# Causal attention in a fused two-layer block: the later keys masked on TensorE, the second half of the queries first, its rough maxima one group ahead

## The chip, the core and the metric

The kernel is one program on one core of one Trainium2 chip. The engines named below are PE (TensorE, matrix products into PSUM), DVE (VectorE), ACT (ScalarE), POOL (GpSimd) and SP (SyncE, which here issues DMAs). The metric is the device time of one execution in microseconds; shorter is better. "Before" is the kernel without the change.

## What is computed

The program runs a mixture of experts, attention, a mixture of experts, a low-rank layer, a second attention of another kind, and a low-rank layer, each added to the running rows `x`. The change touches the first attention alone. Its input is 2 sequences of 1024 tokens with 256 features, 16 heads of 16 features:

```python
q = (x @ Wq).reshape(B, T, H, Dh)            # B, T, H, Dh = 2, 1024, 16, 16
k = (x @ Wk).reshape(B, T, H, Dh)
v = (x @ Wv).reshape(B, T, H, Dh)
scores = jnp.einsum('bthd,bshd->bhts', q, k)
scores = scores * mask                       # mask = tril of ones
attn = jax.nn.softmax(scores / T ** 0.5, axis=-1)
out = jnp.einsum('bhts,bshd->bthd', attn, v).reshape(B, T, H * Dh)
return out @ Wo
```

The mask multiplies. A later key has the score 0, not minus infinity, and so still has a weight in the softmax.

## The kernel before

`attention_stage` works in 8 groups `G` (`NG`): 4 heads (`HG`) of one sequence. Queries are taken in two halves `q` of 512 (`HB`), keys in 8 tiles `j` of 128 (`P`, `TB`). A group is a hand-written loop of 24 slots `s` (`NSL`). Slot `s` handles key tile `s // 2` in the order of `key_of` for one pair of heads: `scores_of` (L984) makes the scores with keys on the partitions, ACT takes the exponential (`exp_of`, L1149) into `PT`, POOL zeroes the part above the diagonal (`cut_later_keys`, L861), and at every odd slot `values_of` (L1002) adds the key tile's values into PSUM bank 6. The first query half has 4 key tiles (slots 0 to 7), the second 8 (slots 8 to 23). Each key tile of a half that crosses the diagonal uses fewer of the 512 queries (512, 384, 256, 128).

The exponential needs the maximum of each query over its keys. It comes from a rough pass over the same products with the queries on the partitions: `rough_scores` (L963) makes a piece of up to 512 columns in bank 0 or 1 in turn, and `maxima` on DVE (L1258, L1260) reduces it; PE may be two pieces ahead. A piece that ends on the diagonal is multiplied by a mask row `SEEN` while it is reduced, one head at a time (L1258); a piece wholly below the diagonal is a plain `tensor_reduce` (L1260). A group has 40 pieces, 12 for its first half and 28 for its second. `per_slot` says how many stand in a slot: slots 8 to 23 of group G make the first half of group G+1 and 16 pieces of its second half, slots 0 to 5 of group G+1 the 12 that are left. Then for each half: `block_max` on DVE (L1270 to L1273), four transposes on PE (`max_rows`, L972) into bank 7 (`MISC`), and copies of four rows into `QT` (`max_copies`, L1132 on ACT, L1280 on DVE), which let `scores_of` subtract the maximum inside the product. For the first half this stands in slots 16 and 17 of the group before; for the second half in slot 6 of its own group, and slot 8 is the first that needs it.

`MISC` is also used by projections (L946), by filler work in the slots of `FILL` (transposes and values of the second sequence, the output projection of the first) and by `out_transposes` (L1010). Each user waits until the reader of the last one is done (`misc`).

The queries and keys of a group are projected two groups ahead, split into a high and a low part (`high`, `low`), and SP places the 16 rows of each head into `QT` and `KT` with DMAs (L835). Group 0 has 24 DMAs of 512 tokens, every later group 12 of 1024 tokens, from the end of the group two before. DVE clears the maximum rows of `QT` for the next group in slots 7 and 14 (`clear_max_rows`, L1286), four `memset`s a group. Ahead of group 0, in the prologue, the first 28 pieces of group 0 run alone; after group 7 the output rows of the second sequence are projected.

Each engine runs its instructions in the order in which they are written; semaphores are the only link between engines.

## Time and profile before

| what | us |
|---|---|
| median of 3 runs | 2196.66 |
| lowest and highest of the 3 | 2193.28, 2201.62 |
| the profiled execution | 2202.58 |
| its span, first to last instruction | 2200.8 |
| groups 0 to 7 of the attention, 339.25 to 712 of the span | 372.8 |

The rows further down come from the profiled execution. A time in a row is counted from the start of the span; `<-` in square brackets names what ended the idle time before an instruction, `x4` how many like it follow each other. A matmul's time in a row includes the time until its end is visible, so matmuls that follow each other overlap: the distance of two starts is what one costs. PEclk is the granted share of TensorE's full clock; the records hold two levels of it, 1.2 and 2.4 GHz.

### The profile page before, as it was taken

To read this page: it belongs to the slowest core of one execution; us is meant where nothing else is said; L and a number is where in the kernel's file an instruction comes from. 1 tells how busy PE (TensorE), PEld (TensorE's weight loads), DVE (VectorE), ACT (ScalarE), POOL (GpSimd) and SP (SyncE) were. 2 spreads that over 40 slices of the span, in tenths; PEclk is the share of its full clock that TensorE was granted. 3 is DMA by queue.
4 is the path that set the end of the run, shared out by engine and by line. 5 is a ranking of instruction groups with operands and counts; after the bars stand their busy time and mean duration, and the time that the engine had idled before them with its cause. 6 is when DMAs were issued, how large, how long until landed. Compare 5 with 4: busy or idle time off the path is not lost. (4 is left out here: it accounts for less than half of the span.)

```text
span 2200.8 us, 29601 instructions
## 1 busy us (share of the span) xinstructions
PE 1992.3 (91%) x8700; PEld 1251.4 (57%) x8700; DVE 1277.8 (58%) x3064; ACT 817.6 (37%) x1549; POOL 866.3 (39%) x684
## 2 busy tenths in 40 slices
PE   5899869898888789977689999999999999999987
PEld 5676635554554766656545555555565555555556
DVE  6322275777775822227556666666656666667526
ACT  2122244555555212223224444444514444444423
POOL 0344301231212044432025555665425555565632
PEclk9999968999899689998669999999999999999999
DMA  9111232232220811224232212222122222211101
GB/s 389 48 63 63 56 124 29 30 48 39 29 30 1 339 62 60 67 72 155 47 72 58 54 42 51 57 57 57 23 64 58 53 58 57 55 44 47 31 1 51
DMA packets 60587, 150.91 MB, mean 69 GB/s; under 512 B 12976, under 2 KB 18304, under 8 KB 58176
## 3 DMA queue, kind: packets, MB, share of 16 engines
q1 hardware_dynamic: 50208, 120.43, 20.9%
q0 software_dynamic: 9120, 24.92, 3.6%
q10 hardware_dynamic: 1152, 4.19, 0.5%
q8 instruction: 60, 0.98, 0.2%
q14 instruction: 47, 0.39, 0.1%
HBM read 68.95 MB, written 18.61 MB: 40 GB/s over the span
## 5 line engine op out<-in xcount | busy, mean ns | idle before, releaser
L1843 POOL TENSOR_TENSOR mla_PS<-mla_PS,mla_PT 128x1024 f32<-128x1024 f32 x192 | 458.1, 2386 | 199.5 <-ACT mla_PT L2129 198.1
L2272 DVE TENSOR_REDUCE mla_MXP<-PS 128x1 f32<-128x512 f32 x512 | 334.6, 687 | 200.5 <-PE PS L1924 198.3
L2129 ACT ACTIVATE mla_PT<-PS 128x512 f32<-128x512 f32 x512 | 293.5, 599 | 420.6 <-PE PS L1944 372.5
L1953 PE MATMUL PS<-mla_PT,mla_CN 128*64 128x512 f32 x1024 | 274.2, 614 | 0.0
L522 DVE COPY moe_HT<-PS 128x256 f32<-128x256 f32 x188 | 70.7, 418 | 301.5 <-PE PS L648 301.5
L1924 PE MATMUL PS<-mla_KH,mla_QH 113*128 113x512 f32 x512 | 199.4, 456 | 18.1 <-DMA mla_KL<-mla_SL 17.9
L1944 PE MATMUL PS<-mla_QH,mla_KH 113*128 113x512 f32 x512 | 210.2, 411 | 1.7 <-ACT mla_QH L2113 1.5
L1944 PE MATMUL PS<-mla_QH,mla_KL 113*128 113x512 f32 x512 | 201.8, 394 | 0.0
L1944 PE MATMUL PS<-mla_QL,mla_KH 113*128 113x512 f32 x512 | 201.7, 394 | 0.0
L684 POOL DMA_INDIRECT moe_XS<-rows_in,moe_GI x96 | 93.5, 974 | 268.3 <-PE PS L634 132.0
L1149 ACT ACTIVATE att_PT<-PS 128x1024 f32<-128x1024 f32 (+1 forms) x192 | 152.1, 812 | 94.3 <-PE PS L984 92.7
L1924 PEld LDWEIGHTS PS<-mla_KH,mla_QH 113*128 113x128 f32 x512 | 91.3, 194 | 168.2 <-DVE mla_MXP L2272 89.7
L641 PE MATMUL PS<-W,moe_ST 128*128 x376 | 174.9, 608 | 1.9 <-DVE moe_ST L516 1.9
L656 PE MATMUL PS<-W,moe_HT 128*128 x752 | 173.7, 384 | 1.4 <-DVE moe_HT L522 1.4
L1843 POOL TENSOR_TENSOR mla_PS<-mla_PT 128x1024 f32<-128x1024 f32 x32 | 76.3, 2384 | 249.1 <-ACT mla_PT L2129 249.1
L963 PE MATMUL PS<-att_KT,att_QT 128*128 128x512 f32 (+3 forms) x384 | 145.6, 423 | 22.6 <-DVE att_MX L1260 10.1
L656 PEld LDWEIGHTS PS<-W,moe_HT 128*128 128x128 f32 x752 | 138.9, 190 | 22.8 <-issue 1.8
L1258 DVE CUSTOM_DVE_ANT_0 PS<-PS,att_SEEN 128x128 f32<-128x128 f32 (+3 forms) x256 | 122.8, 508 | 46.9 <-PE PS L963 44.3
L861 POOL TENSOR_SCALAR_AFFINE_SELECT att_PT<-att_PT 128x256 f32<-128x256 f32 x128 | 51.9, 406 | 244.6 <-ACT att_PT L1149 244.6
L2284 DVE RECIPROCAL PS<-PS 128x128 f32<-128x128 f32 x128 | 108.7, 918 | 52.3 <-PE PS L1960 52.3
L1944 PEld LDWEIGHTS PS<-mla_QH,mla_KH 113*128 113x128 f32 x512 | 96.4, 188 | 68.3 <-issue 22.0
L963 PEld LDWEIGHTS PS<-att_KT,att_QT 128*128 128x128 f32 x384 | 74.7, 210 | 100.5 <-DVE att_MX L1260 38.5
(295 smaller groups left out, 3188.8 us busy)
## 6 DMA issues: line engine op xcount, KB each, us to landing
W<-in_W_dram SPq DMA_DIRECT2D x16, 2048.0 KB, 27.9
mla_QH<-mla_SH SPq DMA_DIRECT2D x64, 128.0 KB, 2.4
mla_KH<-mla_SH SPq DMA_DIRECT2D x64, 128.0 KB, 2.4
mla_QL<-mla_SL SPq DMA_DIRECT2D x64, 128.0 KB, 2.5
mla_KL<-mla_SL SPq DMA_DIRECT2D x64, 128.0 KB, 2.4
mla_KH<-mla_SH SPq DMA_DIRECT2D x64, 96.0 KB, 2.3
mla_KL<-mla_SL SPq DMA_DIRECT2D x64, 96.0 KB, 2.4
sums_Y<-rows_out SPq DMA_DIRECT2D x9, 512.0 KB, 6.2
```

The source lines that it names most:

```text
L641: ins = pe.matmul(bank(2 + u)[:, :], ST[:, u, k, :], g.W1[:, expert, k, :], start=(k == 0), stop=(k == KD - 1))
L656: ins = pe.matmul(bank(6 + u)[:, 0:D], HT[:, u, k, :], W2[:, expert, k, :], start=(k == 0), stop=(k == KF - 1))
L963: ins = pe.matmul(out[:, m, :], QT[:, H % 2, h, i * P:(i + 1) * P], KT[:, H % 2, h // 2, k0:k0 + w], start=(m == 0), stop=(m == len(hs) - 1))
L1149: act.activation(PT[:, kk % 2, 2 * pair:2 * pair + 2, c0:HB], st_banks(s)[:, :, c0:HB], ACT.Exp, scale=SEQ ** -0.5).then_inc(s_p.handle, 1)
L1258: ins = dve.tensor_tensor_reduce(part, part, seen, 1.0, LEAST, ALU.mult, ALU.max, MX[:, q, c, h, t:t + 1])
L1843: pool.tensor_tensor(PS[:, :], PT[:, slot(0), :] if k == 1 else PS[:, :], PT[:, slot(k), :], ALU.add).then_inc(s_ps.handle, 1)
L1924: pe.matmul(bank(piece_bank(n))[:, :], QH[USED, buf, h, tile * P:(tile + 1) * P], KH[USED, buf, h, c * HB:(c + 1) * HB], start=True, stop= ...
L1944: ins = pe.matmul(bank(st_bank(s, h))[:, :], kk[USED, buf, h, ks], qq[USED, buf, h, qs], start=(n == 0), stop=(n == 2))
L1953: ins = pe.matmul(bank(6)[h * DKVL:(h + 1) * DKVL, :], CN[:, b, k, 0:DKVL], PT[:, slot(k), h * HB:(h + 1) * HB], start=(k == 0), stop=(k = ...
L2129: act.activation(PT[:, slot(k), h * HB:(h + 1) * HB], bank(st_bank(s, h))[:, :], ACT.Exp, scale=MLA_SCALE).then_inc(s_p.handle, 1)
L2272: dve.tensor_reduce(MXP[:, n // NPC, c, h, t:t + 1], bank(piece_bank(n))[:, :], AX_X, ALU.max).then_inc(s_mx.handle, 1)
L2284: dve.reciprocal(bank(A)[:, cols], bank(A)[:, cols]).then_inc(s_rc.handle, 1)
```

## The change

- Masking. `SEEN` goes. PE adds to each diagonal piece a product of an identity (`IDR`) with a matrix `LATER` that is 0 or -1e30, over the last 128 columns of each head, into the same bank. DVE reduces every piece with one plain `tensor_reduce`, over 4 heads (128 columns each), 2 heads (256) or 1 head at once. A group has 38 pieces, 11 and 27.
- Order. Slots 0 to 15 take the second query half (all 8 key tiles), slots 16 to 23 the first half. The pieces of the second half of group G+1 stand in slots 6 to 20 of group G, those of its first half in slots 21 to 23 and in its own slots 0 to 5. `block_max`, `max_rows` and `max_copies` of the second half stand in slots 21 and 22 of the group before, those of the first half in slots 7, 8 and 9 of its own group; slots 0 and 16 need them.
- Other places. The projections move from slots 18 and 20 to 12 and 14, the first half's output transposes from slot 11 to 19, the filler slots to 3, 6, 10, 16, 18, 21, and POOL's sums for the second sequence (`later_tiles(1)`) from slot 14 to slot 18 of group 2.
- Rows. SP places every group's rows by halves, 24 DMAs of 512 tokens. From group 2 on the second half goes after slot 16, the first half after slot 24 of the group two before. The rough scores of the second half wait for 18 of the 24, group 0's too.
- Clearing moves from DVE to POOL: slot 17 for the second half of two groups on, slot 3 for the first half of the next.

```diff
-    NROW = 16 * 6 * 2
+    NROW = 16 * 6
...
+    HALF = (1, 0)
+    pieces = [(q,) + p for q in HALF for p in pieces_of_block(q)]
...
-    FROM = 8
-    per_slot = {s: 2 for s in range(FROM, NSL)} | {s: 1 for s in range(FROM + 4, FROM + 8)} | {s: 2 for s in range(6)}
+    FROM = 6
+    per_slot = {s: 2 for s in range(FROM, 21)} | {s: 1 for s in (6, 12, 14)} | {21: 1, 22: 1, 23: 1} | {0: 1, 1: 2, 2: 1, 3: 2, 4: 1, 5: 1}
...
-    key_of = lambda kk: (0, kk) if kk < 4 else (1, kk - 4)
+    key_of = lambda kk: (1, kk) if kk < TB else (0, kk - TB)
...
-    FILL = (3, 6, 9, 13, 15, 22)
+    FILL = (3, 6, 10, 16, 18, 21)
...
-        return (G + 2, (18, 20).index(s)) if s in (18, 20) and G + 2 < NG else None
+        return (G + 2, (12, 14).index(s)) if s in (12, 14) and G + 2 < NG else None
...
-                    if G >= 2:
-                        sp.wait_ge(s_st.handle, s_st.at(NSL * (G - 1)))
-                    for half in range(2 if G == 0 else 1):
...
+                    for half in HALF if G else (0, 1):
+                        if G >= 2:
+                            sp.wait_ge(s_st.handle, s_st.at(NSL * (G - 2) + 2 * TB if half else NSL * (G - 1)))
+                        tok = slice(half * HB, (half + 1) * HB)
+                        for dst, at, high_rows, low_rows in ((KT, 64, (0, 33), (16,)), (QT, 0, (0, 16), (33,))):
+                            s_placed = s_first if half == 0 and dst is QT else s_rows
...
+                def clear_max_rows(H, r):
+                    q = HALF[r]
+                    pool.wait_ge(s_st.handle, s_st.at(NSL * (H - 1) if r else NSL * (H - 2) + 2 * TB))
...
+                    for e in range(2):
+                        pool.memset(f32(QT[max_row(e), H % 2, e:HG:2, q * HB:(q + 1) * HB]), 0.0).then_inc(s_zero.handle, 1)
...
-                        if (G, s) == (2, 14):
+                        if (G, s) == (2, 18):
                             later_tiles(1)
...
-                            pe.wait_ge(s_first.handle, s_first.at(NROW))
-                        elif n == (NPC0 if H == 0 else 0):
-                            pe.wait_ge(s_rows.handle, s_rows.at(NROW * (H + 1)))
...
+                        if n == 0:
+                            pe.wait_ge(s_rows.handle, s_rows.at(3 * NROW * (H + 1)))
+                        if n == NPC1:
+                            pe.wait_ge(s_first.handle, s_first.at(NROW * (H + 1)))
...
+                        masked = k0 + w == (i + 1) * P
...
+                        if masked:
+                            ins = pe.matmul(out[:, :, w - P:w], IDR[:, :], bcast(LATER[:, :], 1, len(hs)), start=False, stop=True)
...
-                        if s == 6:
+                        if s == 8:
                             max_rows(G, 1)
-                        if s == 17 and G + 1 < NG:
+                        if s == 22 and G + 1 < NG:
                             max_rows(G + 1, 0)
...
-                                ins = dve.tensor_tensor_reduce(part, part, seen, 1.0, LEAST, ALU.mult, ALU.max, MX[:, q, c, h, t:t + 1])
...
+                        part = bank(n % 2)[:, 0:len(hs) * w].rearrange("p (h k) -> p h k", k=w)
+                        ins = dve.tensor_reduce(MX[:, q, c, hs[0]:hs[-1] + 1, t], part, AX_X, ALU.max)
```

PE, group 5 before, from slot 5 to slot 8 (the brackets name the semaphores waited for; `att_piece_max` comes from DVE's maxima, `att_max_rows` from the copies into `QT`):

```order
L963 MATMUL PS<-att_KT,att_QT 128x512 [waits att_piece_max]
L984 MATMUL PS<-att_QT,att_KT 128x128 [waits att_probs]
L984 MATMUL PS<-att_QT,att_KT 128x128
L972 MATMUL PS<-C,att_MB 128x128 [waits att_block_max,att_out_sum]
L972 MATMUL PS<-C,att_MB 128x128 x3
L1016 MATMUL PS<-C,att_AO 128x128 [waits att_out_rows,att_max_rows]
L1016 MATMUL PS<-C,att_AO 128x128
L984 MATMUL PS<-att_QT,att_KT 128x128 [waits att_probs]
L984 MATMUL PS<-att_QT,att_KT 128x128
L1002 MATMUL PS<-att_PT,att_VV 32x256 [waits att_later_keys_cut]
L1002 MATMUL PS<-att_PT,att_VV 32x256 x3
L984 MATMUL PS<-att_QT,att_KT 128x512 [waits att_probs,att_max_rows]
```

PE in the changed kernel, group 5, from slot 21 to slot 0 of group 6 (L1002 are the transposes of the maxima, L1014 the scores, L991 the rough scores, L994 the mask, L1032 the values, L1052 a filler):

```order
L994 MATMUL PS<-att_LATER,att_IDR 128x512
L1032 MATMUL PS<-att_PT,att_VV 32x384 [waits att_later_keys_cut]
L1032 MATMUL PS<-att_PT,att_VV 32x384 x3
L1052 MATMUL PS<-att_Wo,att_AT 128x256 [waits att_outrowsT_copied,att_out_sum]
L1052 MATMUL PS<-att_Wo,att_AT 128x256
L1014 MATMUL PS<-att_QT,att_KT 128x128 [waits att_probs]
L1014 MATMUL PS<-att_QT,att_KT 128x128
L1002 MATMUL PS<-C,att_MB 128x128 [waits att_block_max,att_x_updated]
L1002 MATMUL PS<-C,att_MB 128x128 x3
L991 MATMUL PS<-att_KT,att_QT 128x256 [waits att_piece_max]
L991 MATMUL PS<-att_KT,att_QT 128x256
L994 MATMUL PS<-att_LATER,att_IDR 128x2x128
```

The transposes of the maxima no longer have the maxima of the same slots ahead of them and the scores that need them two slots on: here two slots with rough scores, scores and values stand between them and slot 0, and the first half's have eight slots.

DVE before, the same place of group 5 (L1295 to L1298 finish the output of the half before, L1272 and L1273 are `block_max`):

```order
L1258 ISA PS,att_MX<-PS,att_SEEN 128x512 [waits att_rough_scores]
L1258 ISA att_MX 128x1
L1295 TENSOR_TENSOR att_F<-PS,att_F 128x256 [waits att_out_rows,att_later_part,att_out_in_psum]
L1296 TENSOR_TENSOR att_D<-PS,att_D 128x16
L1298 RECIPROCAL att_RC<-att_D 128x16 [waits att_out_sum]
L1272 SCALAR_TENSOR_TENSOR att_MB<-att_MX 128x4x3 [waits att_later_weight,att_maxT_in_psum,att_piece_max]
L1273 SCALAR_TENSOR_TENSOR att_MB<-att_MX,C 128x4
L1280 CAST att_QT<-PS 1x512 [waits att_maxT_in_psum]
L1280 CAST att_QT<-PS 1x512
L1286 MEMSET att_QT 1x2x512 [waits att_max_rows,att_scores]
L1286 MEMSET att_QT 1x2x512
```

DVE in the changed kernel, slots 15 to 22 of a group (L1283 are all maxima, L1303 the copies):

```order
L1283 TENSOR_REDUCE att_MX<-PS 128x1 [waits att_rough_scores] x12
L1312 TENSOR_TENSOR att_F<-PS,att_F 128x256 [waits att_out_rows,att_later_part,att_out_in_psum]
L1313 TENSOR_TENSOR att_D<-PS,att_D 128x16
L1315 RECIPROCAL att_RC<-att_D 128x16 [waits att_out_sum]
L1295 SCALAR_TENSOR_TENSOR att_MB<-att_MX 128x4x3 [waits att_later_weight,att_maxT_in_psum,att_piece_max]
L1296 SCALAR_TENSOR_TENSOR att_MB<-att_MX,C 128x4
L1283 TENSOR_REDUCE att_MX<-PS 128x4 [waits att_rough_scores]
L1303 CAST att_QT<-PS 1x512 [waits att_maxT_in_psum]
L1303 CAST att_QT<-PS 1x512
L1283 TENSOR_REDUCE att_MX<-PS 128x2 [waits att_rough_scores] x2
```

The `memset`s are gone from DVE, the diagonal pieces are plain reductions, and one piece of the next half stands between `block_max` and the copies.

## Rows read from the trace of the kernel before

**Rows 1.** The page's part 1: busy us, share of the span, instructions.
```profile
PE 1992.3 (91%) x8700; PEld 1251.4 (57%) x8700; DVE 1277.8 (58%) x3064; ACT 817.6 (37%) x1549; POOL 866.3 (39%) x684
```

**Rows 2.** Windows of groups 1, 5, 7; behind a stall in group 5: us, busy per engine, PEclk, DMA.
```profile
392.85:440.24 47.39, 42.37 (x236) 23.94 (x234) 35.76 (x99) 25.59 (x40) 12.81 (x25) 0.96 0.26 34
...
584.84:632.70 47.86, 42.41 (x229) 24.09 (x228) 36.91 (x103) 24.41 (x36) 9.23 (x22) 0.93 0.25 33
...
676.92:712.00 35.08, 30.95 (x189) 16.01 (x187) 13.21 (x35) 21.40 (x31) 9.40 (x23) 0.90 0.00 1
...
597.60:604.40 6.80, 6.22 (x32) 4.31 (x33) 4.37 (x15) 3.51 (x7) 1.78 (x4) 0.50 0.00 1
```

**Rows 3.** Timeline of PE, group 5, slots 6 and 7: start us, us.
```profile
594.12 0.33 PE L984 MATMUL PS<-att_QT,att_KT 128*128 128x128 f32 x2
596.04 0.63 PE L972 MATMUL PS<-C,att_MB 128*128 128x128 f32 x4 [1.59 <-DVE att_MB L1273]
598.18 0.69 PE L1016 MATMUL PS<-C,att_AO 128*128 128x128 f32 x2 [1.51 <-DVE att_QT L1280]
```

**Rows 4.** Timeline of DVE in the same place.
```profile
596.71 1.41 DVE L1280 CAST att_QT<-PS 1x512 fp32r<-1x512 f32 x2 [0.81 <-PE PS L972]
```

**Rows 5.** Waits of PE's matmuls, 340 to 712: us in total, times, longest.
```profile
PE PS L972 <- DVE att_MB L1273: 12.3, 8, 1.6
PE PS L963 <- DVE att_MX L1260: 8.1, 25, 0.8
...
PE PS L963 <- DVE att_MX L1258: 4.7, 16, 0.5
```

**Rows 6.** Waits of PE's weight loads, 340 to 712.
```profile
PEld PS L963 <- DVE att_MX L1260: 32.7, 53, 1.2
PEld PS L963 <- DVE att_MX L1258: 25.6, 49, 0.8
```

**Rows 7.** DVE by line and form, 340 to 690: busy us, mean ns, idle before.
```profile
L1260 DVE TENSOR_REDUCE att_MX<-PS 128x1 f32<-128x512 f32 x116 | 77.0, 688 | 14.4 <-PE PS L963 13.3
...
L1286 DVE MEMSET att_QT<- 1x1024 f32 x24 | 21.9, 912 | 6.4 <-issue 6.4
L1258 DVE CUSTOM_DVE_ANT_0 PS<-PS,att_SEEN 128x128 f32<-128x128 f32 x56 | 15.3, 316 | 15.2 <-PE PS L963 15.2
```

**Rows 8.** Timeline of PE at full clock: four 128-column, then two 512-column matmuls.
```profile
560.87 0.60 PE L1010 MATMUL PS<-C,att_OT 128*128 128x128 f32 x4
...
568.23 0.40 PE L963 MATMUL PS<-att_KT,att_QT 128*128 128x512 f32 x1
568.46 0.62 PE L984 MATMUL PS<-att_QT,att_KT 128*128 128x512 f32 x2
```

**Rows 9.** PE by line and form, 340 to 712: busy us, mean ns.
```profile
L972 PE MATMUL PS<-C,att_MB 128*128 128x128 f32 x60 | 9.3, 277 | 12.3 <-DVE att_MB L1273 12.3
L1010 PE MATMUL PS<-C,att_OT 128*128 128x128 f32 x60 | 9.0, 273 | 0.0
```

**Rows 10.** Timeline of SP: last DMA issue of group 0, first and last of group 1.
```profile
308.86 0.59 SPq L835 DMA_DIRECT2D att_QT<-att_SL  x1
...
346.23 0.56 SPq L835 DMA_DIRECT2D att_QT<-att_SH  x1
...
353.20 0.59 SPq L835 DMA_DIRECT2D att_QT<-att_SL  x1
```

**Rows 11.** DMA issues, 280 to 720: count, KB each, median us to landing.
```profile
att_QT<-att_SL SPq DMA_DIRECT2D x14, 128.0 KB, 7.1
...
att_QT<-att_SL SPq DMA_DIRECT2D x4, 64.0 KB, 2.2
```

**Rows 12.** Timeline of PE: prologue, its end, and slot 6 of group 0.
```profile
308.16 1.29 PE L963 MATMUL PS<-att_KT,att_QT 128*128 128x256 f32 x4 [3.77 <-DVE att_MX L1258]
...
331.16 1.05 PE L935 MATMUL PS<-att_VV,att_SLOW 128*128 128x256 f32 x2
...
352.53 0.33 PE L984 MATMUL PS<-att_QT,att_KT 128*128 128x128 f32 x2
```

**Rows 13.** POOL by line and form, whole span: busy us, mean ns.
```profile
L852 POOL TENSOR_TENSOR att_VS<-att_VS,att_VV 128x256 f32<-128x256 f32 x10 | 7.3, 731 | 0.8
L1413 POOL MEMSET mla_GK<- 64x1152 f32 x1 | 1.1, 1051 | 1.7 <-POOLq L361 1.7
```

More of the change, by code:

```diff
@@ L55 @@
 NLAT = DQL + DKVL
[L56 removed]
+LEAST, UNSEEN = -3.0e38, 1.0e30
 MLA_SCALE = float(HD1 + RD) ** -0.5
@@ L732, in pieces_of_block @@
                 out += [(t, c, c * HB, HB, (h,)) for h in range(HG)]
-            if rest <= 2 * P:
-                out += [(t, whole, whole * HB, rest, (h, h + 2)) for h in range(2)]
+            if rest == P:
+                out.append((t, whole, whole * HB, rest, tuple(range(HG))))
+            elif rest == 2 * P:
+                out += [(t, whole, whole * HB, rest, (h, h + 1)) for h in range(0, HG, 2)]
             else:
@@ L737, in pieces_of_block @@
         return out
-    pieces = [(q,) + p for q in range(2) for p in pieces_of_block(q)]
+    HALF = (1, 0)
+    pieces = [(q,) + p for q in HALF for p in pieces_of_block(q)]
     NPC = len(pieces)
-    NPC0 = sum(1 for p in pieces if p[0] == 0)
-    FROM = 8
-    per_slot = {s: 2 for s in range(FROM, NSL)} | {s: 1 for s in range(FROM + 4, FROM + 8)} | {s: 2 for s in range(6)}
-    assert sum(per_slot.values()) == NPC and sum(per_slot[s] for s in range(FROM, FROM + 8)) == NPC0
+    NPC1 = sum(1 for p in pieces if p[0] == 1)
+    FROM = 6
+    per_slot = {s: 2 for s in range(FROM, 21)} | {s: 1 for s in (6, 12, 14)} | {21: 1, 22: 1, 23: 1} | {0: 1, 1: 2, 2: 1, 3: 2, 4: 1, 5: 1}
+    assert sum(per_slot.values()) == NPC and sum(per_slot[s] for s in range(FROM, 21)) == NPC1
     ordered = list(range(FROM, NSL)) + list(range(0, 6))
@@ L768, in attention_stage @@
     filler = {(n // 6, FILL[n % 6]): x for n, x in enumerate(second)}
-    filler |= {(n // 6 + 2, FILL[n % 6]): ("later", n - 5) for n in range(5, 13)}
-    filler |= {(NG0 + n // 4, FILL[1 + n % 4]): x for n, x in enumerate(first_out)}
+    filler |= {(n // 6 + 2, FILL[n % 6]): ("later", n - 6) for n in range(6, 14)}
+    filler |= {(NG0 + n // 4, FILL[2 + n % 4]): x for n, x in enumerate(first_out)}
     assert len(filler) == 5 * TB
@@ L823, in _ @@
                         sp.wait_ge(s_afill.handle, s_afill.at(2 * (G + 1)))
[L824 to L835 removed]
+                    for half in HALF if G else (0, 1):
[4 more added lines that the diff above has]
+                            s_placed = s_first if half == 0 and dst is QT else s_rows
+                            for src, s_made, rows in ((SH, s_hi, high_rows), (SL, s_lo, low_rows)):
+                                sp.wait_ge(s_made.handle, s_made.at(2 * G + half + 1))
+                                for e in range(2):
+                                    for row in rows:
+                                        to, made = 64 * e + row, at + 2 * DH0 * e
+                                        part = slice(e, HG, 2) if dst is QT else slice(0, 2)
+                                        sp.dma_start(f32(dst[to:to + DH0, G % 2, part, tok]), src[made:made + 2 * DH0, tok]).then_inc(s_placed.handle, 16)
                 sp.wait_ge(s_w.handle, s_w.at(48))
@@ L1057, in _ @@
                 pe.wait_ge(s_c.handle, s_c.at(3))
-                rough_scores(0, range(NPC0))
+                rough_scores(0, range(NPC1))
                 max_rows(0, 0)
-                rough_scores(0, range(NPC0, begin[0]))
                 for t in range(TB):
@@ L1280, in max_copies, with sums @@
                         dve.tensor_copy(QT[max_row(h), G % 2, h, q * HB:(q + 1) * HB], MISC[VW * h:VW * h + 1, :]).then_inc(s_nm.handle, 1)
-                def clear_max_rows(H, q):
-                    dve.wait_ge(s_st.handle, s_st.at(NSL * (H - 1)))
-                    dve.wait_ge(s_nm.handle, s_nm.at(8 * (H - 1)))
-                    for e in range(2):
-                        dve.memset(f32(QT[max_row(e), H % 2, e:HG:2, q * HB:(q + 1) * HB]), 0.0).then_inc(s_zero.handle, 1)
-                def sums(G, q):
-                    n = 2 * G + q
+                def sums(G, r):
+                    n = 2 * G + r
                     u = MISC[:, :].rearrange("p (t h d) -> p t h d", t=4, d=VW)
@@ L1315, in _ @@
                 dve.wait_ge(s_afill.handle, s_afill.at(4))
-                maxima(0, range(NPC0))
+                maxima(0, range(NPC1))
                 block_max(0, 0)
                 max_copies(0, 0)
-                maxima(0, range(NPC0, begin[0]))
                 for G in range(NG):
```

125 lines of the change are left out of this document (62 added, 63 removed).

## The prediction

> **What bounds the kernel now.** I read the page's busy shares first [rows 1]: PE has 91 per cent, an average over stages, so the attention has to be read alone. The windows give 47.39 us for group 1 and 47.86 us for group 5, with PE busy 42.4, DVE 36 to 37 and POOL 9 to 13 us [rows 2]. PE bounds a group, but not all the time. Next I looked at the timeline of PE for its longest holes [rows 3]. Behind the scores of slot 6 it waits 1.59 us for `block_max`, makes four transposes, and waits 1.51 us for the copies into `QT`, because the next user of `MISC` may not start before them. DVE's two copies take 1.41 us behind those transposes [rows 4]. The waits show that this happens in each of the 8 groups: 12.3 us in 8 for the first hole [rows 5]; with 1.51 for the second that is 12.3/8 + 1.51 = **3.05 us a group**.
>
> Behind this place the granted clock is 0.50 of full, the lower of its two levels, for 6.80 us of group 5 [rows 2]; over the whole group it is 0.93, in group 1 0.96. So 0.07 x 47.86 = 3.35 and 0.04 x 47.39 = 1.9 us of full clock are lost; the mean 2.6 times PE's busy share (42.4/47.6 = 0.89 to 0.91 near the stall) makes **2.4 us a group**.
>
> The third is where PE waits for DVE's maxima: 8.1 + 4.7 us for matmuls [rows 5], that is 1.6 a group. The weight loads wait 32.7 + 25.6 us [rows 6], 7.3 a group, much of it while earlier matmuls still run.
>
> **The change part by part.** *The stall.* The transposes of the maxima now have two slots between them and the scores that need them, and `block_max` has two slots or more of PE's work ahead of its reader. I take away 3.05 us. What is late next is the copies ahead of slot 0: DVE's take 1.41 us from the end of the transposes [rows 4], with one maximum of 0.69 possibly ahead of them, while PE makes a slot and a half of rough scores, scores and values, about 1.7 us by starts 0.23 us apart for 512 columns [rows 8] plus the values. That is even; I count 0.5 us for the new tight place (bounds 0 and the old 3.05).
>
> *The clock.* The 6.80 us at half clock behind the stall are the whole loss of group 5 (6.80 x 0.50 = 3.4 [rows 2]). I take it as the stall's consequence: 2.4 us back (bounds 0 and 3.2).
>
> *The masks.* A group gets 22 matmuls more, one on each diagonal piece: 2 over four heads (4 x 128 = 512 columns), 4 over two heads (256), 16 over one head (128). Starts lie 0.23 us apart at 512 [rows 8]; at 128 four transposes take 0.60 us, the last 0.27 of it [rows 8, 9], so (0.60 - 0.27)/3 = 0.11; for 256 I take 0.12, near 128 since a weight load stands between. 2 x 0.23 + 4 x 0.12 + 16 x 0.11 = **2.7 us**. From below: where PE would wait for DVE anyway, up to 1.6 us [rows 5] are absorbed, so 1.1. From above: each exposed with its 0.27 visible end [rows 9], 22 x 0.27 = 5.9. I stay at 2.7, since PE runs such matmuls back to back.
>
> Here a row and a page differ. The row shows 0.11 and 0.23 us from start to start [rows 8, 9]. The Trainium skill ("TensorE: Matmul & The Clock Gate", section "Back-to-back issue gap") has streams of matmuls with their weight loads at some 81 ns for 128 columns and 131 ns for 512. By the page, as an estimate, the masks would cost about 0.8 us a group less, some 6 us in the whole; the trace doesn't agree, and its number decides.
>
> *DVE.* Sixteen heads of 128 columns took 16 x 0.316 = 5.1 us, now four plain reductions of the same 512 columns at 0.688 make 2.8 [rows 7]: 2.3 less, and next to nothing for the other widths. The four `memset`s of a group, 0.91 each and 0.27 idle ahead of each (6.4/24) [rows 7], leave too: 4.7. DVE's work falls by 7.0 of 36.9 us. Where PE waits for DVE now, the maxima end earlier. Of 1.6 (matmuls) to 7.3 us a group (loads) I take **2.0**, by the matmul row, because a load that waits beside a running matmul costs nothing; low end 0.
>
> *Groups 1 to 6:* -3.05 - 2.4 + 2.7 - 2.0 + 0.5 = -4.25, six times **-25.5 us**.
>
> *Group 7* makes only the last 8 pieces of its own first half, with 8 masks of 0.11: -3.05 - 3.2 (0.10 x 35.08 x 0.91 [rows 2]) + 0.9 - 1.2 = **-6.5**.
>
> *Group 0.* Its loop starts at 339.25. The rough scores of group 1 now begin in slot 6 and wait for 18 of the 24 DMAs. SP issues the first at 346.23 and 12 of them in 353.20 - 346.23 = 6.97 us, so 0.634 apart [rows 10]; the 18th goes out at 346.23 + 17 x 0.634 = 357.0 and lands 2.2 us later by the 64 KB row [rows 11], at 359.2. PE reaches slot 6 at 352.53 [rows 12]. That is a **new wait of 6.7 us**, with scores of slot 7 and all behind it queued (bounds 4, with POOL and masks ahead of slot 6 slowing PE, and 11.6 if 64 KB takes the 7.1 us of the 128 KB row [rows 11]). The low clock behind it I leave as before. -3.05 + 6.7 + 2.7 - 1.0 + 0.5 = **+5.9**.
>
> *Prologue.* 27 pieces of the second half replace 28, and all 24 DMAs must have landed first: 308.86 + 0.59 + 2.2 = 311.7 [rows 10, 11], against PE at 308.16, which was itself waiting 3.77 us for DVE [rows 12]. From there 27 pieces at DVE's pace, 16 plain of 0.69 and 11 of about 0.65 with some 2.5 us of waits, 20.7, and `block_max` and transposes 2.0 end at 334.4; the sums now start at 331.16 [rows 12]. **+3** (bounds 0 and 6).
>
> *POOL.* The clears move there. A `memset` of 64x1152 took 1.05 us on POOL [rows 13], against 0.91 of 1024 on DVE [rows 7]; POOL is busy 9 to 13 of 47 us, so they are hidden, except in group 2: two clears in slot 17 (2.1 us) and six sums of 0.73 (`later_tiles(1)`) [rows 13] in slot 18 stand ahead of the cut that the values of slot 19 to 21 need. 2.1 + 4.4 - about 4.2 of slots passed is **+2.3** (bounds 0 and 6.5).
>
> The rows above price a POOL `memset` at nearly DVE's time [rows 7, 13]. [...]
>
> *At nothing:* SP's 24 issues a group, 15.2 us of 47; the first half of the rows is due after slot 24 and needs 6 x 0.634 + 2.2 = 6.0 us, while slot 6 is some 10 us away. If it lands in 7.1, 0.9 us a group come up. The projections and fillers change places, not number; the cover is PE's own work.
>
> **Sum:** -25.5 - 6.5 + 5.9 + 3 + 2.3 = **-20.8**. The profiled execution took 2202.58, so 2181.8 there; it lies 5.9 above the median of the runs, 2196.66, to which I apply the sum: **2176 us**.
>
> **The rivals.**
> *A, the masks are exposed.* Each waits for the piece before it and shows its whole 0.27 us [rows 9]: 5.9 - 2.7 = 3.2 a group, seven times 22, so 2198, no change. Against it: 128-column matmuls follow each other at 0.11 [rows 8].
> *B, slower: the stall moves to the end of the group.* Slots 21 to 0 hold `block_max`, transposes and copies, one after the other on DVE and PE. If DVE is still behind by 1.5 us or more at slot 21 (the last maximum of the 27 pieces late), PE waits for `block_max`, then at slot 0 for the copies, as it does now in slots 6 and 7 [rows 3], and the low clock stays too. Six groups lose 3.05 + 2.4 again and group 7 its 6.2: -20.8 + 32.7 + 6.2 = +18, so 2215. It decides from a DVE delay of some 1.5 us. Against it: DVE has 7 us less to do.
> *C, the rows come late.* 64 KB land in 7.1 us: 4.9 in group 0 and 0.9 in six groups, +10.3, so 2186. For it: 24 DMAs at a time rather than 12.
> *D, DVE was the real bound* where loads wait: 5.2 instead of 2.0 a group [rows 6], -19, so 2157.
> *E, the clock stays low* somewhere in each group for another hole: 2.4 x 6 + 3.2 = 17.6 back, so 2194, no change.
>
> **How the numbers follow.** Forecast with small variants, C among them: 0.62. D 0.08. A and E, within 0.5 per cent, 0.21. B 0.09. About 0.5 per cent, 11 us, is what a measurement of this kernel can tell from no change: faster is below 2185.7, slower above 2207.6. The range 2160 to 2200 takes in A, C and E and the ends of the masks and of group 0, and leaves out B and most of D, under 2 in 10. Faster 0.70, same 0.21, slower 0.09.
>
> **What the changed profile would show.** Right: no holes of 1.5 us ahead of the transposes of the maxima in slots 8 and 22, PEclk near 1.0 over groups 1 to 6, a period of 42 to 44 us, starts 0.11 to 0.23 us apart at the masks, one hole of 6 to 7 us in slot 6 of group 0 that ends on a DMA, DVE busy near 29 us a group, the first rough scores at about 312. Wrong: a hole at slots 22 to 0 that ends on DVE (B), a slope of the period with the number of masks (A), low clock without a hole (E), a hole on DMA in each slot 6 (C), or a hole ahead of the values in group 2 longer than 2.3 us.

## The result, and the profile after

The changed kernel takes **2178.49 us** (median of 5 runs, 2178.26 to 2180.11); the kernel before, with two more runs, 2201.62 (5 runs, 2193.28 to 2204.16). The ratio is 0.990, with a 95 per cent interval of 0.9885 to 0.9914: faster by 23.1 us, about one per cent. 2176 was forecast. Between the two profiled executions (2202.58 and 2178.26) the difference is 24.3 us, and the prediction's sum was 20.8.

The windows of groups 0, 1, 2, 5 and 7 answer to [rows 2]: us, busy time of PE, PEld, DVE, ACT and POOL with the number of instructions, PEclk, DMA. Behind them stand groups 0 and 2 of the kernel before.

```profile
342.76:400.21 57.45, 48.79 (x265) 29.17 (x263) 30.76 (x54) 26.95 (x43) 11.74 (x22) 0.94 0.18 42
400.21:443.88 43.67, 42.29 (x257) 25.82 (x256) 29.81 (x54) 26.01 (x41) 16.62 (x29) 1.00 0.16 37
443.88:491.18 47.30, 43.36 (x251) 26.20 (x250) 31.26 (x55) 25.72 (x39) 20.20 (x36) 0.93 0.15 35
...
580.57:623.28 42.71, 41.24 (x251) 24.91 (x251) 31.32 (x58) 24.47 (x37) 12.99 (x26) 1.00 0.16 38
...
662.68:692.38 29.70, 27.69 (x192) 15.10 (x192) 10.81 (x23) 21.58 (x32) 10.01 (x24) 1.00 0.00 1
```

```profile
339.25:392.85 53.60, 47.64 (x232) 27.10 (x231) 32.23 (x93) 26.89 (x43) 11.54 (x22) 0.90 0.23 30
...
440.24:487.70 47.46, 42.34 (x233) 23.74 (x232) 36.08 (x99) 25.43 (x39) 15.91 (x30) 0.96 0.26 34
```

Group 1 goes from 47.39 to 43.67, group 5 from 47.86 to 42.71, group 7 from 35.1 [rows 2] to 29.7. PE is as busy as before (42.3 and 41.2 against 42.4), but it now is busy for 97 per cent of the group, and the granted clock is 1.00. DVE has 6 us less. Two groups stand out: group 0 is longer than before (57.45 against 53.60), and group 2, at 47.30, gained nothing; its clock is 0.93.

The waits of PE's matmuls from 342 to 693 say why (us in total, times, longest), against [rows 5]:

```profile
PE PS L991 <- DVE att_MX L1283: 7.5, 28, 0.5
PE PS L991 <- DMA att_KT<-att_SL: 6.5, 1, 6.5
PE PS L1032 <- POOL att_PT L868: 3.9, 2, 2.8
PE PS L1002 <- DVE X L1320: 1.0, 3, 0.3
```

The wait of the transposes for `block_max` (12.3 us in 8) is gone, and so are the waits of 1.5 us for the copies [rows 3], which in the kernel before added up to 12.0 us in 8:

```profile
PE PS L1016 <- DVE att_QT L1280: 6.0, 4, 1.5
...
PE PS L927 <- DVE att_QT L1280: 4.5, 3, 1.5
PE PS L935 <- DVE att_QT L1280: 1.5, 1, 1.5
```

What longer waits remain are one for a DMA, in slot 6 of group 0, and one for POOL, in group 2 (2.8 us; the other 1.1 of the 3.9 stand at the end of group 7). The weight loads hardly gained: 51.7 us in 86 waits for DVE, against 58.3 in [rows 6].

Over the whole loop the granted clock is 0.98 where it was 0.94: before, TensorE is at half clock for 47.8 us of the loop, in every group; now for two stretches of 6.8 us, behind the two long waits.

```profile
339.25:712.25 373.00, 331.92 (x1804) 187.72 (x1802) 262.51 (x732) 197.32 (x300) 86.84 (x188) 0.94 0.23 30
```

```profile
342.76:692.38 349.62, 327.61 (x1973) 198.36 (x1971) 224.38 (x404) 198.72 (x300) 108.19 (x211) 0.98 0.14 33
...
361.30:368.10 6.80, 4.05 (x12) 2.71 (x16) 1.00 (x3) 1.03 (x2) 0.00 (x0) 0.50 0.39 89
...
484.10:490.90 6.80, 5.21 (x30) 3.38 (x30) 2.44 (x5) 2.13 (x5) 3.44 (x8) 0.50 0.00 0
```

The whole divides as follows. The loop took 373.0 us and takes 349.6 (-23.4); the prologue ends 3.5 us later, at 342.76; the rest of the program, whose code is the same, took 1488.6 and takes 1484.1 (-4.4). For that last part no cause in the change is known: in the kernels below it lies between 1480.6 and 1490.8 without any order. So I compare loops by their traces below, and the medians stand beside them. The start of a loop holds the code ahead of the attention too, which is the same in all: the attention's first product on PE comes at 285.06 us in the changed kernel, and between 283.6 and 287.7 in those of the table.

### The profile page after: what moved, and what is told of

It is laid out like the page before. It is cut to its first block and busy times, and to the rows that moved or that the text cites. A ratio compares the mean times of both kernels' runs of the same rounds, so it can differ in the third digit from the quotient of the medians.

```text
span 2176.5 us, 29726 instructions
## 1 busy us (share of the span) xinstructions
PE 1987.0 (91%) x8876; PEld 1261.1 (58%) x8876; DVE 1238.4 (57%) x2704; ACT 818.4 (38%) x1549; POOL 888.6 (41%) x708
## 5 line engine op out<-in xcount | busy, mean ns | idle before, releaser
L1283 DVE TENSOR_REDUCE att_MX<-PS 128x1 f32<-128x512 f32 (+3 forms) x304 | 194.3, 660 | 86.2 <-PE PS L994 47.5
L991 PE MATMUL PS<-att_KT,att_QT 128*128 128x512 f32 (+3 forms) x384 | 141.9, 414 | 24.7 <-DVE att_MX L1283 9.2
L656 PEld LDWEIGHTS PS<-W,moe_HT 128*128 128x128 f32 x752 | 138.9, 190 | 23.4 <-issue 2.6
L700 POOL DMA_INDIRECT rows_out<-moe_YS,moe_DI x94 | 93.0, 989 | 84.5 <-ACT moe_YS L560 75.0
```

The source lines that it names most:

```text
L656: ins = pe.matmul(bank(6 + u)[:, 0:D], HT[:, u, k, :], W2[:, expert, k, :], start=(k == 0), stop=(k == KF - 1))
L991: ins = pe.matmul(out[:, m, :], QT[:, H % 2, h, i * P:(i + 1) * P], KT[:, H % 2, h // 2, k0:k0 + w], start=(m == 0), stop=(m == len(hs) - ...
L1283: ins = dve.tensor_reduce(MX[:, q, c, hs[0]:hs[-1] + 1, t], part, AX_X, ALU.max)
```

## Experiments: the parts one by one

| kernel | median us (range) | loop from, us | loop, us | group 1 | group 2 | group 5 | group 6 |
|---|---|---|---|---|---|---|---|
| before | 2201.62 (2193.28 to 2204.16) | 339.25 | 373.0 | 47.4 | 47.5 | 47.9 | 44.2 |
| changed | 2178.49 (2178.26 to 2180.11) | 342.76 | 349.6 | 43.7 | 47.3 | 42.7 | 39.4 |
| masks back on DVE | 2179.37 (2178.45 to 2182.41) | 345.03 | 344.9 | 43.1 | 46.2 | 42.1 | 38.8 |
| masks made twice | 2196.37 (2193.17 to 2202.35) | 344.05 | 363.6 | 45.8 | 48.1 | 44.8 | 41.7 |
| the tight place put back | 2207.88 (2203.78 to 2211.56) | 344.24 | 379.3 | 46.0 | 51.2 | 47.8 | 44.4 |
| clears back on DVE | 2194.33 (2190.59 to 2199.65) | 345.56 | 371.7 | 48.6 | 48.1 | 47.9 | 39.9 |
| masks and clears back (order only) | 2199.03 (2192.47 to 2203.39) | 340.87 | 365.8 | 48.2 | 47.8 | 46.2 | 39.6 |
| before, clears on POOL | 2213.86 (2205.83 to 2221.70) | 338.66 | 384.6 | 50.1 | 49.1 | 50.2 | 45.5 |
| before, masks on PE | 2208.10 (2204.17 to 2211.79) | 338.97 | 383.1 | 49.9 | 48.1 | 49.1 | 46.6 |

A group's length is from its first scores to the next group's, in the profiled execution. That one execution lies between 4.7 us below the median of its kernel (with both repairs, further down) and 5.3 above it (clears back on DVE); how far a loop differs from one execution to the next was not measured. The kernel before took between 2200.0 and 2201.9 us in the medians beside these runs.

**The tight place.** Stall and clock were the two largest terms, so they came first: everything as changed, but the transposes of the first half's maxima again where the next slot needs them.

```diff
-                        if s == 8:
-                            max_rows(G, 1)
...
+                        if s == 15:
+                            max_rows(G, 1)
...
-                        if s == 7:
-                            block_max(G, 1)
-                        if s == 9:
-                            max_copies(G, 1)
...
+                        if s == 15:
+                            block_max(G, 1)
+                            max_copies(G, 1)
```

> The changed kernel with the old tight place put back: block_max, transposes and copies of the first half's maxima all stand at the end of slot 15, one slot ahead of the scores that need them (slots 7, 8 and 9 in the changed kernel). Theory: the two holes of PE come back, about 3 us in each of 8 groups, and behind them PE's granted clock falls to half for 3.4 to 6.8 us in the groups where it was full: 8 x 3 + 7 x 2.4 = +41, 2219 us. Rival 1 (the holes come back, the clock has another cause): +24, 2202, with a granted clock of 1.00 in groups 3 to 7. Rival 2 (with the shorter work of DVE the place isn't tight any more): below +8, 2186.

The loop grew by 29.7 us. PE's waits in it, and the windows of groups 1 and 5 (columns as above):

```profile
PE PS L1014 <- DVE att_QT L1303: 12.1, 8, 1.5
PE PS L1002 <- DVE att_MB L1293: 7.1, 7, 1.0
```

```profile
406.41:452.44 46.03, 42.34 (x256) 25.81 (x257) 29.90 (x54) 26.00 (x41) 16.63 (x29) 1.00 0.15 35
...
600.63:648.44 47.81, 44.04 (x251) 26.77 (x251) 31.66 (x58) 24.69 (x37) 13.00 (x26) 0.93 0.15 34
```

Both holes are back, 12.1/8 + 7.1/7 = 2.5 us a group. Group 1 kept its full clock and grew by 2.4 us, the holes alone; group 5 fell to 0.93 and grew by 5.1. So the holes of a group are worth 2.5 and the clock that may fall behind them another 2.6, and the same holes do not always bring the clock down: it was at half for 6.8 us behind them in groups 4, 5 and 6, for 3.4 in groups 0 and 2, and not at all in 1 and 3. The expected 41 was too much by that, and because the hole ahead of the transposes is 1.0 us where it was 1.5. The result, 2207.88, lies between the theory (2219) and rival 1 (2202): the holes bring the clock down with them, but not in every group.

**The masks.** One kernel leaves them on DVE, one makes them twice.

```diff
-                        masked = k0 + w == (i + 1) * P
...
-                        if masked:
-                            ins = pe.matmul(out[:, :, w - P:w], IDR[:, :], bcast(LATER[:, :], 1, len(hs)), start=False, stop=True)
...
+                                ins = dve.tensor_tensor_reduce(part, part, seen, 1.0, LEAST, ALU.mult, ALU.max, MX[:, q, c, h, t:t + 1])
```

> The changed kernel with the masking alone undone: DVE multiplies by the mask row SEEN again, one head at a time, and PE makes no mask products; order, rows and clearing stay changed. Theory (the sum of the prediction): PE saves 2.7 us a group, DVE gets 2.3 back of which a third costs time, so about -2.0 us in seven groups, -14, 2164 us against 2178.5 of the changed kernel. Rival 1 (DVE bounds the pieces, so the masks paid for themselves): the weight loads of the rough scores wait longer for DVE, between 0 and +16 us, 2178 to 2195. Rival 2 (the masks were exposed): -6 us a group, 2137.

```diff
+                            for last in range(2):
+                                ins = pe.matmul(out[:, :, w - P:w], IDR[:, :], bcast(LATER[:, :], 1, len(hs)), start=False, stop=(last == 1))
```

> The changed kernel with each mask product made twice: 22 more matmuls a group, everything else alike. Theory: one set costs what was summed, 2.7 us in seven groups, +19, 2197 us. Rival 1 (PE waits for DVE there anyway): +1.1 a group or less, 2179 to 2186. Rival 2 (each exposed with its 0.27 us): 5.9 a group, 2220.

The median came out as the theory had it (2197), but the loop grew by only 14.0 us, 2.1 in group 1. The loop holds seven and a half sets of masks (120 products of 128 columns, 16 in a set): 14.0/7.5 = **1.9 us a group**, not 2.7 (2.0 if counted as seven, as the expectations below do). A timeline of PE in group 4 of the changed kernel shows a single mask:

```profile
573.78 0.40 PE L991 MATMUL PS<-att_KT,att_QT 128*128 128x512 f32 x1
574.03 0.22 PE L994 MATMUL PS<-att_LATER,att_IDR 128*128 128x128 f32 x1
574.09 0.47 PE L991 MATMUL PS<-att_KT,att_QT 128*128 128x512 f32 x1
```

From one piece of 512 columns to the next it is 0.31 us with the mask, and 0.23 without [rows 8], so 0.08 for the mask; from the start of the mask to the next start it is 0.06. At the median of the loop that distance is 0.06 for 128 columns, 0.12 for 256 and 0.29 for 512, and 16, 4 and 2 of them make 2.0 us, near the 1.9 of the doubled set. The four transposes from which I took 0.11 were the wrong neighbour. The Trainium skill ("TensorE: Matmul & The Clock Gate", section "Back-to-back issue gap") has some 81 ns for 128 columns, nearer to these rows than the 0.11; its 131 ns for 512 columns does not agree with the 0.23. I had set its figure aside for the transposes.

Without masks on PE the loop is only 4.8 us shorter. If one set costs what the second cost, DVE's shorter maxima gave back 14.0 - 4.8 = 9.2 us, 1.2 a set. The loop starts 2.3 us later, but the attention's first product comes 2.7 later too (287.74 against 285.06), so the prologue itself didn't grow. By the loop, moving all masks to PE cost 4.8 us; by the median it gained 0.9 (2179.37), and in the profiled execution the part behind the attention took 6.6 us more. The theory (-14) did not come out. Rival 1 did by its two signs: the median lies in its range (2178 to 2195), and the weight loads of the rough scores wait longer for DVE, 68.6 us instead of 51.7. By the loop, -4.8, the truth lies between the two.

```profile
PEld PS L990 <- DVE att_MX L1283: 42.4, 74, 1.1
PEld PS L990 <- DVE att_MX L1285: 26.2, 43, 1.3
```

**The clears.** The changed kernel with the four `memset`s a group back on DVE:

```diff
+                        if s == 4 and 2 <= G + 1 < NG:
+                            clear_max_rows(G + 1, 1)
+                        if s == 18 and G + 2 < NG:
+                            clear_max_rows(G + 2, 0)
```

> The changed kernel with the clearing alone put back on DVE: four memsets a group, two in slot 4, two in slot 18. Theory: DVE's 4.7 us a group cost the share that the sum gave to them, 1.3 us in six groups, +8, less about 1 us because POOL is free sooner in group 2: 2185 us. Rival 1 (DVE has slack, nothing was won by taking the clears away): 2176 to 2180. Rival 2 (they stand ahead of block_max and the copies and delay the scores of slot 0): +4.7 in six groups, 2206.

It cost 22.1 us of the loop and 15.8 of the median, two to three times what the sum gave to DVE's relief by them (8), and so between the theory (2185) and rival 2 (2206). The timeline of DVE and then of PE at slot 18 of group 5, and PE's window behind it, show how:

```profile
633.04 0.91 DVE L1292 MEMSET att_QT<- 1x1024 f32 x1 [0.27 <-issue]
634.22 0.91 DVE L1292 MEMSET att_QT<- 1x1024 f32 x1 [0.27 <-issue]
635.16 1.29 DVE L1265 TENSOR_REDUCE att_MX<-PS 128x1 f32<-128x512 f32 x2
```

```profile
633.30 0.59 PE L996 MATMUL PS<-att_QT,att_KT 128*128 128x384 f32 x2
635.91 0.80 PE L973 MATMUL PS<-att_KT,att_QT 128*128 128x512 f32 x1 [2.02 <-DVE att_MX L1265]
```

```profile
635.40:642.20 6.80, 6.29 (x24) 4.01 (x25) 3.27 (x6) 0.60 (x1) 0.41 (x1) 0.50 0.05 10
```

Two clears keep DVE for 2.4 us; PE may be only two pieces ahead, so it stands for 2.02, and 6.80 us at half clock follow. The changed order has a piece in every slot, so the clears hold up maxima here; slots other than 4 and 18 were not tried. In the kernel before, slots 6 and 7 have no piece, and the clear of slot 7 fell there.

**The order alone.** With masks and clears both back on DVE (rows by halves and the other new places stay, and were not tried apart):

> The changed kernel with masking and clearing both back on DVE: what is left of the change is the order, the rows by halves and their places. Undoing the masking alone made the attention loop 4.8 us shorter (344.85 against 349.61), undoing the clearing alone 22.1 longer (371.73). Theory (the two add up): a loop near 367, 2192 us. Rival 1 (with both on DVE, DVE bounds the pieces, and its work counts in full): 2.3 more in seven groups, a loop near 385, 2210, slower than before. Rival 2 (the order alone brings the gain): below 2183.

Its edits are those of the two kernels above together. It took 2199.03 us, a ratio to before of 0.9985 (0.9972 to 0.9998): nearly nothing of the gain. Waits of PE, and the window of group 1:

```profile
PE PS L972 <- DVE att_MX L1267: 20.4, 27, 2.2
PE PS L972 <- DMA att_KT<-att_SL: 6.9, 1, 6.9
PE PS L972 <- DVE att_MX L1265: 5.7, 18, 0.7
PE PS L993 <- DVE att_QT L1287: 1.7, 7, 0.3
```

```profile
400.42:448.60 48.18, 42.79 (x235) 23.24 (x235) 35.36 (x100) 26.02 (x41) 12.90 (x25) 0.96 0.15 34
```

The waits for `block_max` and the copies are gone, as the order meant, but 26.1 us of waits for maxima stand in their place (12.8 in [rows 5]), and the clock of group 1 is 0.96 as before. So the order takes the stall away from one place and DVE's 35.4 us of work open it in another. The loop (365.8) is near the 367 of adding the two parts, so these two do add from the changed side, as far as single executions can tell: the medians add to 2195.2, 3.8 us below the measured one, and that is 7 us above its forecast.

**The clears alone**, on POOL in the old order and in the old slots:

```diff
-                        if s in (7, 14) and 2 <= G + 1 < NG:
-                            clear_max_rows(G + 1, (7, 14).index(s))
...
+                    pool.wait_ge(s_cut.handle, s_cut.at(NCUT * (H - 1) + cuts(8)))
...
+                        pool.memset(f32(QT[max_row(e), H % 2, e:HG:2, q * HB:(q + 1) * HB]), 0.0).then_inc(s_zero.handle, 1)
```

> The kernel before with one part of the change alone: the four clears of a group go from DVE to POOL, in the same slots 7 and 14; masking, order and rows as before. Theory (in the old order the clear of slot 7 falls in the two slots without rough pieces, so less hangs on it than in the changed order): between 0 and -7 us against before, 2194 to 2201, the holes of slots 6 and 7 and the low clock stay. Rival (the clears cost as much as in the changed order, where undoing them gave back 15.8 us): -16, 2185.

Slower than before by 0.57 per cent (0.41 to 0.74), against every expectation. The timeline of POOL and of PE in slots 7 and 8 of a group:

```profile
558.71 0.41 POOL L861 TENSOR_SCALAR_AFFINE_SELECT att_PT<-att_PT 128x256 f32<-128x256 f32 x1 [4.33 <-ACT att_PT L1163]
559.31 1.94 POOL L877 MEMSET att_QT<- 1x1024 f32 x2 [0.20 <-POOL att_PT L861]
```

```profile
559.16 1.22 PE L998 MATMUL PS<-att_QT,att_KT 128*128 128x512 f32 x2
561.36 1.09 PE L977 MATMUL PS<-att_KT,att_QT 128*128 128x128 f32 x4 [0.97 <-issue]
```

On POOL the clears queue behind the cut of slot 7, which waits 4.33 us for its exponential, and end at 561.25; the first rough piece of the next group, in slot 8, waits for them by its semaphore (the profile names no releaser there, "issue") and starts at 561.36. In 6 groups such holes add up to 7.8 us of the 11.6 by which the loop grew, as the waits of PE have it; the granted clock over the loop is 0.92 where it was 0.94:

```profile
PE PS L977 <- issue: 7.8, 6, 2.0
```

In the changed kernel the split by halves lets the clears go half a group or more ahead of their reader (slots 17 and 3), and no wait of PE ends on them there. Whether another slot of POOL would do in the old order was not tried.

**The masks alone**, on PE in the kernel before, with its pairs of heads:

```diff
-                        if k0 + w == (4 * q + t + 1) * P:
...
+                        ins = dve.tensor_reduce(MX[:, q, c, hs[0]:hs[-1] + 1:2, t], part, AX_X, ALU.max)
```

> The kernel before with another part alone: PE makes the masks (24 products a group, heads in the old pairs), DVE reduces every piece plainly; order, rows and clearing as before. Theory: a mask set costs 2.0 us a group on PE as the doubled set showed, DVE's shorter work gives 1.3 of it back, +0.7 in eight groups, 2206 us. Rival 1 (the shorter maxima bring block_max forward and shorten the hole ahead of the transposes in slot 6): -0.7 a group or more, 2195 or less. Rival 2 (DVE gives nothing back): +2.0 in eight groups, 2217.

2208.10, slower by 0.26 per cent (0.15 to 0.38), as the theory had it (2206), though the loop grew by 10.1 us; the hole ahead of the transposes stayed at 12.2 us in 8. So each part done alone does nothing or harm (0.9985, 1.0057, 1.0026), and the three together give 0.990.

## Experiments: the two new waits, and a faster version

**Group 2.** POOL's timeline in slots 17 to 20 of group 2 of the changed kernel, and PE's values behind it:

```profile
477.34 1.95 POOL L897 MEMSET att_QT<- 1x1024 f32 x2
...
480.52 0.74 POOL L859 TENSOR_TENSOR att_VS<-att_VV 128x256 f32<-128x256 f32 x1
481.33 3.94 POOL L859 TENSOR_TENSOR att_VS<-att_VS,att_VV 128x256 f32<-128x256 f32 x5
485.23 1.12 POOL L868 TENSOR_SCALAR_AFFINE_SELECT att_PT<-att_PT 128x256 f32<-128x256 f32 x3
```

```profile
485.69 1.51 PE L1032 MATMUL PS<-att_PT,att_VV 128*32 128x384 f32 x8 [2.78 <-POOL att_PT L868]
```

Three cuts wait behind the sums, and PE for them; from 484.1 the clock is at half for 6.80 us. The test does one sum in each of slots 18 to 23:

```diff
-                        if (G, s) == (2, 18):
-                            later_tiles(1)
+                        if G == 2 and s >= 18:
+                            later_tiles(1, (s - 18,))
```

> The changed kernel with POOL's six sums of later_tiles(1) spread over slots 18 to 23 of group 2, one in each, where they all stood in slot 18. Theory: the waits of the values for POOL there (3.9 us in two) go to under 1, and the half clock of 6.8 us behind them goes too: -3.5 - 3 = -6 in group 2, 2172 us against 2178.5. Rival 1 (the low clock there has another cause): -3.5, 2175. Rival 2 (the two clears in slot 17 ahead of the sums make the wait): -1 or less, 2178.

2173.01 us (2171.20 to 2174.60): -5.5, as the theory had it. Group 2 went from 47.30 to 42.17 with a clock of 1.00, and its wait of 2.78 us for POOL is gone. The 1.1 us that the expectation counted with it stand at the end of group 7 and stayed.

**Group 0.** On top of that, the projections of group 1 go into the prologue, so that the rows are placed before slot 6:

```diff
-        if (G, s) in ((0, 0), (0, 1)):
-            return 1, s
...
-                rough_scores(0, range(NPC1))
+                for half in range(2):
+                    rough_scores(0, range(6 * half, 6 * half + 6))
+                    projections(1, half, bank(4 + half))
+                rough_scores(0, range(12, NPC1))
```

> The changed kernel with two repairs: POOL's sums of group 2 spread (e3_sums_spread, 2173.0 us), and the queries and keys of group 1 projected in the prologue, after 6 and 12 of its rough pieces, where they stood in slots 0 and 1 of group 0. Theory: the rows of group 1 are placed before slot 6 of group 0, so the wait of 6.5 us for the DMA goes, with the 6.8 us at half clock behind it (3 us) and the 3.7 us of the two projections, which hide in the prologue where PE waits for DVE: -13, 2160 us. Rival 1 (the prologue grows by what the projections take): -9.5, 2163.5. Rival 2 (another wait, for POOL, DVE or ACT, takes the place of the DMA in slots 1 to 8 of group 0): -4, 2169.

Group 0 fell from 57.5 to 44.9 us, the wait for the DMA is gone and no half clock is left in groups 0 to 7. But the prologue ended at 347.38 instead of 342.56, so the net is -12.5 + 4.8 = -7.7 by the traces (loop 332.3), near rival 1 with the longer prologue. The median, 2168.09 (2163.42 to 2171.55), is only 4.9 us below the 2173.01; the profiled execution is the fastest of the five. By that number rival 2 (2169) is nearest, but its mechanism is not there: no other wait took the place of the DMA, and the longest left in the loop is 1.1 us. With the masks back on DVE as well:

> The same two repairs, and the masking back on DVE with the mask row SEEN. Theory: as in e1_mask_dve the loop gets 4.8 us shorter and the prologue, which runs at DVE's pace, 2.3 longer: 2.5 below e8_both, 2157.5 if that comes to 2160. Rival (the masks only paid where PE waits, and a full clock in all groups makes DVE the bound): 0 to +5 against e8_both.

2171.61 (2163.19 to 2174.34): +3.5, as the rival had it, though the ranges overlap. The loop is 3.6 us shorter (328.6) but starts at 350.04, and 1.8 of these 2.7 us lie ahead of the attention. Then the masks divided: PE masks only the pieces of several heads, where one product serves four or two.

```diff
-                        masked = k0 + w == (i + 1) * P
+                        masked = k0 + w == (i + 1) * P and len(hs) > 1
```

> The same two repairs, and PE masks only the pieces of several heads (3 products for each half of the queries, 6 a group instead of 22), DVE multiplies by SEEN in the pieces of one head. Theory: the 16 products of one head's 128 columns, 0.11 us each, leave PE, 1.8 us a group, and DVE's work hardly grows, since a plain and a masked reduction of one head take nearly the same; so most of the masks' 2.0 us a group comes back: -7 to -12 against e8_both, 2148 to 2153 if that comes to 2160. Rival (DVE's second instruction for each masked head costs what the product cost): within 3 us of e8_both.

2159.58 (2158.36 to 2163.97), 8.5 below the kernel with both repairs, as the theory had it; loop 326.5, 5.7 less than with all masks on PE and 2.1 less than with none. The products that serve four or two heads are worth their price, those for one head are not.

In all of these PE waits 7.6 to 7.7 us at the start of the prologue for the rows of group 0. The last kernel puts the projections of group 1 there:

```diff
+                for half in range(2):
+                    pe.wait_ge(s_lo.handle, s_lo.at(half + 1))
+                    projections(1, half, bank(4 + half))
+                rough_scores(0, range(NPC1))
```

> As e12_mixed (2159.6 us), but both projections of group 1 stand ahead of the first rough piece of the prologue, where PE waits 7.6 us for the DMAs of group 0, and DVE makes the low parts after 4 maxima. Theory: the projections, made at half clock between rough pieces in e12_mixed, fall into that wait, and the loop starts about 3 us earlier, at 344: 2156.5 us. Rival 1 (the prologue runs at DVE's pace, which has the same work as before): 0 to -1. Rival 2 (the longer busy stretch of PE lets the granted clock rise earlier in the prologue): -4 or more.

**2153.24 us** (2151.03 to 2158.39), a ratio to before of 0.9787 (0.9768 to 0.9807). The loop starts at 342.66, 4.6 us earlier, and takes the same 326.5. The timeline of PE in its prologue:

```profile
303.27 3.60 PE L972 MATMUL PS<-att_XT,att_Wqk 128*128 128x512 f32 x8
311.11 1.19 PE L992 MATMUL PS<-att_KT,att_QT 128*128 128x512 f32 x2 [4.24 <-DMA att_QT<-att_SL]
```

Both projections are done inside the wait for the DMA, as the theory had it, but the gain, 6.3 us by the median and 5.9 from the attention's first product to the loop (285.47 to 342.66, where it was 284.18 to 347.24), is in the range of rival 2 (-4 or more). Part of it goes with the clock: one stretch of 27.3 us at half clock stands in this prologue, where the kernel of 2159.58 has three, of 13.6, 3.4 and 13.6 us.

```profile
309.90:337.20 27.30, 22.57 (x44) 11.36 (x44) 20.76 (x41) 7.67 (x8) 2.81 (x4) 0.50 0.26 60
```

So the fastest version has the order and the clears of the change, 6 of its 22 masks a group, and two repairs.

## Why the prediction held, step by step

The mechanism held: the holes of slots 6 and 7 and the low clock behind them are gone, and PE is busy for 97 per cent of a group. That the number came within 3 us is in part luck, since several terms were off and did not weigh on the sum as they were priced.

- **Stall and clock, -5.45 a group: right in place, the size a little off.** 2.5 for the holes and 2.6 for the clock in groups 4 to 6 of the kernel with the tight place (5.1 in all); in groups 1 and 3 the holes alone. But the sum took it as the order's own gain. The order alone gave 7 us of the loop in all, since DVE's load opened new holes. The step that was missing is that this term holds only while DVE keeps up in every slot.
- **The new tight place, +0.5:** no product of PE waited for the copies there; the weight loads of the scores did, 2.9 us in 6.
- **Masks, +2.7: 1.9.** The row for 128 columns was the wrong neighbour; 0.06 to 0.08, not 0.11.
- **DVE's relief, -2.0, "by the matmul row": too small from the changed side.** The masks' part gave 1.2 a set, the clears' part 22.1 us of loop in all (2.4 of DVE's time at a place without slack opened a hole of 2.0 and cost the clock). The price of DVE's time was read from the old order, which has two slots free of pieces; the new one has none. The masks' part of DVE's work was also miscounted: [rows 7] has 56 masked reductions of 128 columns in seven groups, 8 a group and not 16, and the changed kernel takes four heads at once in 2 pieces a group, not 4. DVE's busy time in group 1 is 32.04 us with the masks back and 29.81 without, so the 2.3 less was right by luck.
- **What undoing costs does not add up to the gain.** The tight place put back cost 29.7 us of loop, the clears back on DVE 22.1, and the masks back gained 4.8: 47 in all, but the change gained 23.4. Each of these is the price of new holes in an order that has few left, so the gain cannot be divided among the parts. The two traces can be set side by side instead, as an estimate: PE's waits for maxima, `block_max` and copies fell from 12.8 + 12.3 + 12.0 = 37.1 us to 7.5, new ones of 6.5 and 3.9 came, the half clock fell from 47.8 us to 13.7, some 15 us of PE's work, and the masks cost 14. That makes -20, and 3 stay unexplained.
- Groups 1 to 6 gave -3.7, -0.2, -3.8, -4.0, -5.2 and -4.8, -21.6 in all, against -25.5 + 2.3 = -23.2. Group 7, to its last values (712.25 and 692.38), gave -5.6 (-6.5).
- **Group 0, +5.9: +3.9.** The wait was 6.50 us at the place named (6.7 forecast), ended by the DMA, and the clock behind it was at half for 6.8 us where before it was for 10.2.
- **Group 2, +2.3: right in place, too small.** The hole is 2.78 us, longer than the 2.3 that the prediction had named as a sign of being wrong, and its clock, which the sum had left out, cost another 3. So the group lost some 3.6 us of what its neighbours gained.
- **Prologue, +3: +3.5**, the first rough piece at 310.99 (311.7).
- Loop and prologue together gave -23.4 + 3.5 = -19.9, and the sum was -20.8. The other 4.4 us between the two profiled executions lie behind the attention, in code that is the same.
- The other signs: the clock is 1.00 in five of the groups 1 to 6, and 0.93 in group 2; the period is 42 to 44 us in groups 1, 4 and 5, but 45.4 in group 3 and 39.4 in group 6, both with a full clock.
- The rivals: A's 0.27 us for each mask is excluded by the rows of the mask, and by the doubled set, which A would have put at 2220. B, the stall at slots 22 to 0: not there; the transposes of slot 22 waited 0.35 us at most. C: 64 KB landed in 2.2 us at the median. E happened in one group, 2, behind POOL. D, DVE as the bound, did not come (2157); what holds of it is that DVE's time is worth more than the 2.0 where the order has no slack.
- The base matters little: the first three runs of before had a median of 2196.66, the five 2201.62. From that, the same sum is 2180.8, again within 3 us.

## What to carry to other kernels

A gain from a new order is only as large as the slack of the second engine in it: price every instruction of that engine anew in the new order, above all those that stood in a gap which the new order fills. Parts of a change can each be worthless or harmful alone and worth one per cent together, so undo them one at a time and also do them one at a time. A hole of 1 to 3 us in a busy TensorE can cost the same again in clock behind it, so count both, and look for the few groups that still have one; two such places were worth more here than the masks.

## What the runs showed of the hardware

- Holes of PE and its clock: 6.80 us at 0.50 followed the waits of 6.50 us (group 0), 2.78 (group 2) and 2.02 us (clears on DVE). Behind two holes of 1.0 and 1.5 us in the kernel with the tight place, the clock was at half for 6.8 us in three groups, for 3.4 in two, and stayed full in two others.
- A `memset` of one partition by 1024 took 0.95 us on POOL and 0.91 on DVE, so POOL is hardly slower here; what counts is what it queues behind. The Trainium skill ("GPSIMD Engine Reference", section 4.1 "Engine selection") has GpSimd about twice as slow for operations with two inputs and roughly at line rate for one; it names no operation without an input, and these rows put such a fill at VectorE's pace.
- The part of the program behind the attention, the same code in all, took between 1480.6 us (clears back on DVE) and 1490.8 (masks back on DVE). Why was not tried. That spread, 10.2 us, is as large as most effects here, so a median alone would have misled: the kernel with masks back on DVE has a loop 4.8 us shorter and a median 0.9 longer.
